# Eight heads instead of four in one visit of the causal value products, with two more exponential tiles on top of rows that are loaded later

## The chip, the cores and the metric

One NeuronCore of a Trainium2 chip runs the whole program. The metric is the device time of one execution in microseconds (us), as the median over several executions.

## What is computed

The reference runs a transformer layer with two attentions and a feed-forward part over 16 batches of 256 tokens of width 256, and then a gated attention. The context has 77 tokens. Everything is float32. Cut to what matters here:

```python
# x: (16, 256, 256), ctx: (16, 77, 256); 16 heads of width 16
h = layernorm(x + multihead(x, x, x, sa_wq, sa_wk, sa_wv, sa_wo, causal=True), ln1_g, ln1_b)
h = layernorm(h + multihead(h, ctx, ctx, ca_wq, ca_wk, ca_wv, ca_wo, causal=False), ln2_g, ln2_b)
ff = relu(h @ ff_w1.T + ff_b1) @ ff_w2.T + ff_b2
x = layernorm(h + ff, ln3_g, ln3_b)
qp, kp, vp = x @ Wq + bq, ctx @ Wk + bk, ctx @ Wv + bv
w = softmax(qp @ kp.T / 16)
out = (w @ vp) * mask * sigmoid(concatenate((qp, w @ vp)) @ Wg + bg) + x
```

The change is in the first line, the causal self-attention: softmax(scores / 16) times the values of each head.

## The kernel before

After a first part (context_products, weights and context) one long program, causal_cross_feed_gated, runs three stages that overlap: the causal attention, the cross attention with the feed-forward part, and the gated attention. Each engine has its own instruction list. All five lists are written by walking the same table `order`, and synchronise by semaphores; an engine never leaves the order of its list. There is no scheduler, so what stands behind a waiting instruction waits too.

The causal stage is cut into iterations n, each of 12 slots s, with the running number g = 12 n + s. A batch has 12 units of scores (line 765 adds the causal mask on the diagonal through an identity, L767 multiplies queries and keys, in bfloat16 parts of float32 numbers) and VectorE takes their row maxima (L1405). Later the scores are computed again, turned (keys on the partitions, L791), with the maximum already in the product; ScalarE takes the exponential (L1168) into one of six tiles pT; GpSimd sets the part above the diagonal to zero (L1819); and TensorE multiplies by the values (L809 and L812, in float32, each head on 32 of the 128 columns, four heads side by side). One such group of four heads is called a visit here. Three units of turned scores feed one visit. The lags in slots between a unit's scores and its turned scores, exponential, zeroing and visit are ST_LAG 20, EXP_LAG 21, SEL_LAG 22 and AV_LAG 25.

In one iteration n, besides the scores of batch n and the turned scores of batches n - 2 and n - 1, these are done:

- slot 1: TensorE turns the maxima (L777); ScalarE and VectorE (L1413, slot 2) write them in two parts into the tile a_mT
- slots 3 to 6: projections of queries and keys of batch n + 2 (L87 with swq, swk). The first waits for L1413, since they share the PSUM tile a_misc
- slot 7: ScalarE copies them (L1139), VectorE takes the remainder (L1420) and GpSimd the rest
- slots 9 and 10: projections of values (L87 with swv), which wait for L1420, since they write over the same PSUM tile
- slots 10 and 11: output projection of batch n - 3 (L87 with swo), with the residual on VectorE (L1447) after it
- slots 5 and 11: VectorE turns the value products back (L1429, then the reciprocal L1431), and later, after a product on GpSimd, L1439

The scores, the turned scores and the visits' results have two PSUM tiles each, so the scores of a slot wait for the maxima of two slots before. Exponential g waits until the visit is done that read its tile last.

SyncE issues the loads in a list of its own: for each batch of the causal stage 12 copies that stack the query and key parts; then for batch c of the cross stage the keys (L674), the values (L682, which wait for the last visits of batch 12 + c, since they lie on the same tiles), the queries (L694) and the feed-forward weights (L687, for c up to 3). Cross slots are put beside the causal ones from iteration 12 on. The norm rows (gains and biases of three layernorms, and ff_b2) are seven tiles of 1 KB per partition, loaded once at the start (L178).

The rule on the tiles, word for word:

```python
act.wait_ge(s_st, g + 1)
atleast(act, s_av, (g - NPT) // 3 + 1)
nc.scalar.activation(pT[g % NPT][:], stps[g % 2][:], ACT.Exp).then_inc(s_exp, 1)
```

Of the kernel before, what the change touches and what calls it, by code (L numbers as in the profile page):

```python
# [5 lines left out]
F32 = mybir.dt.float32  # L6
# [7 lines left out]
P = 128  # L14
# [98 lines left out]
def context_products(nc, ctx, sem, t, a, sw, d):  # L113
# [52 lines left out]
    with nc.Block() as block:  # L166
        @block.sync
        def _(sp):
# [8 lines left out]
            for n, v in t.rows.items():  # L177
                sp.dma_start(v[:], A(n).partition_broadcast(P)).then_inc(small, 16)  # L178
# [27 lines left out]
            sp.wait_ge(small, 16 * (len(t.rows) + len(t.cols) + 1 + 2))  # L206

        @block.tensor
        def _(pe):
# [29 lines left out]
            pe.wait_ge(small, 16 * (len(t.rows) + len(t.cols) + 1 + 2))  # L239
# [237 lines left out]
def causal_cross_feed_gated(nc, ctx, sem, t, wq, wk, wv, wo, x_dram, xT_dram, b1, b2, ln1, ln2, ln3, d, w1_dram, w2_dram, out):  # L477
# [6 lines left out]
    NPT, NVP, NPX, NHID = 6, 4, 4, 3  # L484
    ST_LAG, EXP_LAG, SEL_LAG, AV_LAG = 20, 21, 22, 25
# [11 lines left out]
    pT = [sb(f"pT{i}", [P, 512], F32) for i in range(NPT)]  # L497
# [78 lines left out]
    c_loaded = [sem("feed_weights") for _ in range(4)]  # L576
    c_stacked = [sem("c_stacked") for _ in range(NSTK)]
# [73 lines left out]
    with nc.Block() as block:  # L651
        @block.sync
        def _(sp):
# [57 lines left out]
            for c in range(B):  # L711
# [3 lines left out]
                if c >= NSTK:  # L715
                    load_keys(c)
                    load_values(c)
                load_queries(c)
# [33 lines left out]
        def _(pe):  # L752
# [42 lines left out]
            def values(rr):  # L795
                c, r = divmod(rr, 4)
                if not real(c):
                    return
                j, ro = divmod(r, 2)
                if rr == 0:  # L800
                    pe.wait_ge(v_ones, NVP)
                pe.wait_ge(s_sel, 3 * rr + 3)
                if r == 0:
                    pe.wait_ge(s_vev, c + 1)
                if ro == 0:
                    atleast(pe, s_tr, 2 * (c - 1) + j + 1)
                col = ro * S
                for i in range(4):
                    mt(avps[j][32 * i:32 * i + 32, col:col + S], vpad[c % NVP][:, 0, 4 * r + i, :],  # L809
                       pT[(3 * rr + i // 2) % NPT][:, i % 2 * S:i % 2 * S + S], start=True, stop=False, skip_group_check=True)  # L810
                for i in range(4):
                    last = mt(avps[j][32 * i:32 * i + 32, col + P:col + S], vpad[c % NVP][:, 1, 4 * r + i, :],  # L812
                              pT[(3 * rr + 2) % NPT][:, i * P:(i + 1) * P], start=False, stop=True, skip_group_check=True)
                last.then_inc(s_av, 1)
# [41 lines left out]
            def causal_slot(n, s):  # L856
# [12 lines left out]
                if (g - AV_LAG) % 3 == 0:  # L869
                    values((g - AV_LAG) // 3)  # L870
# [920 lines left out]
        def _(pool):  # L1791
# [71 lines left out]
            def shifted_rows2(c):  # L1863
                if not real(c):
                    return
                pool.wait_ge(c_z2r, c + 1)
# [216 lines left out]
```

## Time and profile before

| | before |
|---|---|
| median of 3 runs | 875.87 us (875.33 to 876.85) |
| profiled execution, device time | 875.57 us |
| its span, first to last instruction | 873.8 us |
| TensorE (PE) busy | 787.0 us, 90% |
| VectorE (DVE) busy | 659.1 us, 75% |
| GpSimd (POOL) busy | 485.5 us, 56% |
| ScalarE (ACT) busy | 438.0 us, 50% |
| mean granted TensorE clock | 0.964 |

Busy shares are averages over the stages. The causal stage fills roughly the stretch from 80 to 390 us of the span; its first value product starts at 110.1 us and its last at 391.2. A granted clock of 1.00 is the 2.4 GHz level of TensorE; a lower mean is a mixture with the 1.2 GHz level. The weight loads of TensorE (PEld) are recorded apart from its products. A float32 product stands as two in the trace, so a visit shows as 8 products of L809 and 8 of L812.

### The profile page before, as it was taken

The page shows a single profiled execution, that of the slowest core. Times are in us where ns is not written, and L with a number is a line of the kernel's source. Part 1 is how long each engine was busy: PE and PEld are TensorE (multiplying, and loading weights), DVE is VectorE, ACT ScalarE, POOL GpSimd, SP SyncE. Part 2 cuts the span into 40 slices and gives each one's busy share as a digit, 9 for nine tenths or more (in the row PEclk, how much of TensorE's full clock was granted, in tenths as well). Part 3 has the DMA queues.
Part 4 walks back from the last instruction along what each step waited for, and adds up shares of the span by engine and source line. Part 5 has one row for each costly group of instructions (what it writes and reads, how often), then busy time and mean ns, then how long its engine had stood idle before and what let it go on. Part 6 is the DMA issues. An engine that isn't in the chain of part 4 may idle for free.

```text
span 873.8 us, 19903 instructions
## 1 busy us (share of the span) xinstructions
PE 787.0 (90%) x7214; PEld 651.1 (75%) x7232; DVE 659.1 (75%) x1498; ACT 438.0 (50%) x907; POOL 485.5 (56%) x598
## 2 busy tenths in 40 slices
PE   5896799999999898788789999999999889999895
PEld 4665677777777675555468888888877789989784
DVE  3545767777777989677989999998888776867863
ACT  4431355555565565556555555555544544444442
POOL 2401466677666676554345666666555775657541
PEclk9999999999999999899789999999999999999987
DMA  8397588768765765346432222222200020012122
GB/s 269 60 356 189 108 132 140 139 118 128 131 115 111 115 105 102 76 88 121 79 72 53 54 52 53 53 53 53 53 2 10 2 77 2 28 54 81 54 81 76
DMA packets 105296, 79.58 MB, mean 91 GB/s; under 512 B 43255, under 2 KB 101961, under 8 KB 104941
## 3 DMA queue, kind: packets, MB, share of 16 engines
q1 hardware_dynamic: 101434, 72.02, 39.9%
q10 hardware_dynamic: 3764, 6.29, 2.0%
q8 instruction: 58, 0.95, 0.5%
q14 instruction: 40, 0.33, 0.1%
HBM read 27.03 MB, written 12.97 MB: 46 GB/s over the span
## 4 chain that ended last, share of the span: by engine, by line
PE 61%; DVE 18%; issue 6%; ACT 3%; SPq 1%; DMA 1%; POOL 1%; POOLq 0%; DVEq 0%; ACTq 0%
PE a_misc L87 14%; PE a_pair L87 11%; PE a_s L1002 8%; PE a_pair L963 3%; PE a_pair L791 3%; PE a_s L767 3%; PE a_pair L948 3%; PE a_pair L809 3%; PE a_s L765 2%; PE a_s L87 2%; PE a_s L925 2%; PE a_pair L1101 2%; DVE a_rest L1420 2%; ACT a_parts L1139 2%; DVE c_z L1509 1%
## 5 line engine op out<-in xcount | busy, mean ns | idle before, releaser
L1405 DVE TENSOR_REDUCE a_nm<-a_s 128x2 f32<-128x512 f32 (+1 forms) x192 | 127.5, 680 | 54.9 <-PE a_s L767 53.3
L1912 POOL TENSOR_TENSOR c_hidden<-c_hid,c_hidden 128x256 fp32r<-128x256 f32 x128 | 95.8, 748 | 118.3 <-DVE c_hid L1647 118.2
L1168 ACT ACTIVATE a_pT<-a_pair 128x512 f32<-128x512 f32 x192 | 113.8, 597 | 93.8 <-PE a_pair L791 87.4
L1263 ACT ACTIVATE a_pT<-a_pair 77x512 f32<-77x512 f32 x128 | 75.9, 593 | 141.9 <-PE a_pair L948 137.5
L1002 PE MATMUL a_s<-c_w,c_hidden 128*128 128x256 f32 x768 | 118.6, 294 | 0.0
L87 PE MATMUL a_pair<-c_fxh,c_w 128*128 128x256 f32 x512 | 101.5, 291 | 12.8 <-DVE c_hid L1647 12.8
L1819 POOL TENSOR_SCALAR_AFFINE_SELECT a_pT<-a_pT 128x256 f32<-128x256 f32 (+1 forms) x192 | 91.1, 492 | 30.2 <-ACT a_pT L1168 29.9
L1002 PEld LDWEIGHTS a_s<-c_w,c_hidden 128*128 128x128 f32 x768 | 99.9, 192 | 0.7 <-issue 0.4
L87 PEld LDWEIGHTS a_pair<-c_fxh,c_w 128*128 128x128 f32 x512 | 80.0, 193 | 15.8 <-DVE c_hid L1647 15.6
L791 PE MATMUL a_pair<-a_sq,a_sk 98*128 98x256 bf16 (+1 forms) x512 | 76.0, 252 | 7.3 <-ACT a_pT L1168 7.1
L1647 DVE TENSOR_SCALAR c_hid<-a_pair,ff_b_col 128x256 f32<-128x256 f32 x128 | 61.3, 479 | 28.0 <-ACT c_hidden L1289 27.9
L767 PE MATMUL a_s<-a_sk,a_sq 96*128 96x256 bf16 (+1 forms) x512 | 74.7, 248 | 4.5 <-DVE a_nm L1405 1.8
L87 PE MATMUL a_pair<-c_fxl,c_w 128*128 128x256 f32 x256 | 72.4, 283 | 0.0
L1571 DVE TENSOR_REDUCE a_nm<-a_s 128x5 f32<-128x385 f32 (+1 forms) x96 | 54.5, 568 | 22.8 <-PE a_s L925 21.9
L1289 ACT ACTIVATE c_hidden<-a_pair,ff_b_col 128x256 fp32r<-128x256 f32 x128 | 59.3, 463 | 7.4 <-PE a_pair L87 7.3
L765 PE MATMUL a_s<-maskb,identb 128*128 128x256 bf16 (+1 forms) x174 | 54.0, 310 | 7.5 <-DVE a_nm L1405 7.5
L767 PEld LDWEIGHTS a_s<-a_sk,a_sq 96*128 96x128 bf16 x512 | 45.6, 99 | 11.1 <-issue 0.6
L948 PE MATMUL a_pair<-a_sq,a_sk 98*77 98x256 bf16 x256 | 51.9, 285 | 1.8 <-ACT a_pT L1263 1.8
L87 PEld LDWEIGHTS a_pair<-c_fxl,c_w 128*128 128x128 f32 x256 | 49.3, 193 | 0.0
L791 PEld LDWEIGHTS a_pair<-a_sq,a_sk 98*128 98x128 bf16 x512 | 35.6, 99 | 15.8 <-ACT a_pT L1168 9.7
L925 PEld LDWEIGHTS a_s<-a_sk,a_sq 96*128 96x128 bf16 x512 | 24.3, 102 | 30.1 <-DVE a_nm L1571 14.3
L1827 POOL TENSOR_TENSOR a_on<-a_tr,a_rc 128x256 f32<-128x256 f32 x32 | 21.2, 661 | 44.2 <-DVE a_rc L1431 44.2
(255 smaller groups left out, 2141.2 us busy)
## 6 DMA issues: line engine op xcount, KB each, us to landing
a_sq<-a_parts SPq DMA_DIRECT2D x96, 128.0 KB, 4.4
a_sk<-a_parts SPq DMA_DIRECT2D x96, 128.0 KB, 4.4
a_sq<-c_parts SPq DMA_DIRECT2D x96, 128.0 KB
x<-in_xT SPq DMA_DIRECT2D x16, 256.0 KB, 5.9
res<-in_x SPq DMA_DIRECT2D x16, 256.0 KB, 5.6
out<-g_fin SPq DMA_DIRECT2D x16, 256.0 KB, 2.1
a_sk<-kc_parts SPq DMA_DIRECT2D x96, 38.5 KB
fold_rows<-x_fold ACTq DMA_DIRECT2D x1, 2496.0 KB, 11.3
```

What stands on the lines that cost most here:

```text
L87: last = pe.matmul(out, a(x, kt), b(y, kt), start=start and n == 0, stop=stop and n == len(seq) - 1)
L765: mt(diag, t.identb[:], t.maskb[:, 0:len(heads), :], start=True, stop=False, skip_group_check=True)
L767: last = mt(out[:, i * w:(i + 1) * w], sq[c % NSTK][0:KS, h, qt * P:(qt + 1) * P], sk[c % NSTK][0:KS, h, 0:w], start=False, stop=True, ski ...
L791: last = mt(stps[g % 2][:, i * w:(i + 1) * w], sk[c % NSTK][:, h, kt * P:(kt + 1) * P], sq[c % NSTK][:, h, q0:S], start=True, stop=True, s ...
L948: last = mt(st_ps[0:SC, i * S:(i + 1) * S], skx[c % NSTK][:, h, :], sq[c % NSTK][:, h, :], start=True, stop=True, skip_group_check=True)
L1002: last = mt(down[:, qt * D:(qt + 1) * D], (hh, hl)[x](m)[:, qt * P:(qt + 1) * P], w2(y, m), start=m == 0 and qt == 0 and i == 0, stop=m == ...
L1168: nc.scalar.activation(pT[g % NPT][:], stps[g % 2][:], ACT.Exp).then_inc(s_exp, 1)
L1263: nc.scalar.activation(pT[g % NPX][0:SC], st_ps[0:SC, :], ACT.Exp).then_inc(c_exp, 1)
L1405: nc.vector.tensor_reduce(nm[c % 2][:, QT * heads[0] + qt:QT * heads[-1] + qt + 1:QT], sps[g % 2][:].rearrange("p (h k) -> p h k", h=len(h ...
L1647: nc.vector.tensor_scalar(hid[n % NHID][:], up[n % 2][:, 0:S], b1[:, m:m + 1], 0.0, ALU.add, ALU.max).then_inc(c_hid, 1)
L1819: nc.gpsimd.affine_select(out=v, in_=v, compare_op=ALU.is_ge, fill=0.0, base=0, pattern=[[0, len(heads)], [1, P]], channel_multiplier=-1). ...
L1912: nc.gpsimd.tensor_tensor(hl(m), hid[n % NHID][:], f32(hh(m)), ALU.subtract).then_inc(c_hl, 1)
```

## The change

Two visits become one. values(p) runs every six slots instead of every three and does eight heads: two groups of four, one right after the other, into the two halves of one PSUM tile. AV_LAG grows from 25 to 28, so that the pair stands where the second of the two visits stood, and the six tiles pT become eight. The two new ones lie on the memory of the rows ln2_b with ln3_g and ln3_b with ff_b2. These four rows are no longer loaded at the start, but by SyncE after the last causal value product, in front of the queries of cross batch 3, and GpSimd waits for them once, in shifted_rows2(0).

```diff
-            for n, v in t.rows.items():
-                sp.dma_start(v[:], A(n).partition_broadcast(P)).then_inc(small, 16)
+            for n in t.first_rows:
+                sp.dma_start(t.rows[n][:], A(n).partition_broadcast(P)).then_inc(small, 16)
...
-    NPT, NVP, NPX, NHID = 6, 4, 4, 3
-    ST_LAG, EXP_LAG, SEL_LAG, AV_LAG = 20, 21, 22, 25
+    NPT, NVP, NPX, NHID = 8, 4, 4, 3
+    ST_LAG, EXP_LAG, SEL_LAG, AV_LAG = 20, 21, 22, 28
...
-    pT = [sb(f"pT{i}", [P, 512], F32) for i in range(NPT)]
+    pT = [sb(f"pT{i}", [P, 512], F32) for i in range(NPT - 2)]
+    pT += [nc.alloc_sbuf_tensor_at(f"a_pT{NPT - 2 + i}", [P, 512], F32, offset=t.place[n]) for i, n in enumerate(("ln2_b", "ln3_b"))]
...
+                if c == NSTK - 1:
+                    sp.wait_ge(s_av, 4 * B)
+                    for v, src in t.later_rows:
+                        sp.dma_start(v[:], src.partition_broadcast(P)).then_inc(rows_loaded, 16)
                 load_queries(c)
...
-            def values(rr):
-                c, r = divmod(rr, 4)
-                if not real(c):
-                    return
-                j, ro = divmod(r, 2)
-                if rr == 0:
+            def values(p):
+                c, j = divmod(p, 2)
+                if not real(c):
+                    return
+                if p == 0:
                     pe.wait_ge(v_ones, NVP)
-                pe.wait_ge(s_sel, 3 * rr + 3)
-                if r == 0:
+                pe.wait_ge(s_sel, 6 * p + 6)
+                if j == 0:
                     pe.wait_ge(s_vev, c + 1)
-                if ro == 0:
-                    atleast(pe, s_tr, 2 * (c - 1) + j + 1)
-                col = ro * S
-                for i in range(4):
-                    mt(avps[j][32 * i:32 * i + 32, col:col + S], vpad[c % NVP][:, 0, 4 * r + i, :],
-                       pT[(3 * rr + i // 2) % NPT][:, i % 2 * S:i % 2 * S + S], start=True, stop=False, skip_group_check=True)
-                for i in range(4):
-                    last = mt(avps[j][32 * i:32 * i + 32, col + P:col + S], vpad[c % NVP][:, 1, 4 * r + i, :],
-                              pT[(3 * rr + 2) % NPT][:, i * P:(i + 1) * P], start=False, stop=True, skip_group_check=True)
-                last.then_inc(s_av, 1)
+                atleast(pe, s_tr, p - 1)
+                for ro in range(2):
+                    rr, col = 2 * p + ro, ro * S
+                    for i in range(4):
+                        mt(avps[j][32 * i:32 * i + 32, col:col + S], vpad[c % NVP][:, 0, 8 * j + 4 * ro + i, :],
+                           pT[(3 * rr + i // 2) % NPT][:, i % 2 * S:i % 2 * S + S], start=True, stop=False, skip_group_check=True)
+                    for i in range(4):
+                        last = mt(avps[j][32 * i:32 * i + 32, col + P:col + S], vpad[c % NVP][:, 1, 8 * j + 4 * ro + i, :],
+                                  pT[(3 * rr + 2) % NPT][:, i * P:(i + 1) * P], start=False, stop=True, skip_group_check=True)
+                    last.then_inc(s_av, 1)
...
-                if (g - AV_LAG) % 3 == 0:
-                    values((g - AV_LAG) // 3)
+                if (g - AV_LAG) % 6 == 0:
+                    values((g - AV_LAG) // 6)
...
+                if c == 0:
+                    pool.wait_ge(rows_loaded, 16 * 4)
...
+        t.first_rows = ("ln1_g", "ln1_b", "ln2_g")
+        t.later_rows = [(t.rows[n], a["L0_xattn_" + n]) for n in ("ln2_b", "ln3_g", "ln3_b", "ff_b2")]
```

The instructions of TensorE's list, slots 7, 8 and the start of 9 of an iteration, before. a_s is the PSUM tile of the scores, a_pair that of the turned scores and of the value products, a_pT an exponential tile, a_vpad the values; the last row is the first value projection:

```order
L765 MATMUL a_s1<-maskb,identb 128x2x128
L767 MATMUL a_s1<-a_sk3,a_sq3 128x256 x2
L791 MATMUL a_pair1<-a_sq1,a_sk1 128x128 x4
L809 MATMUL a_pair1<-a_pT0,a_vpad1 32x256 x2
L809 MATMUL a_pair1<-a_pT1,a_vpad1 32x256 x2
L812 MATMUL a_pair1<-a_pT2,a_vpad1 32x128 x4
L765 MATMUL a_s0<-maskb,identb 128x2x128
L767 MATMUL a_s0<-a_sk3,a_sq3 128x256 x2
L791 MATMUL a_pair0<-a_sq2,a_sk2 128x256 x2
L765 MATMUL a_s1<-maskb,identb 128x2x128
L767 MATMUL a_s1<-a_sk3,a_sq3 128x256 x2
L87 MATMUL a_misc<-swv0,a_xh1 128x256
```

And after (line numbers move by six, the visit's lines are now L814 and L817):

```order
L771 MATMUL a_s1<-maskb,identb 128x2x128
L773 MATMUL a_s1<-a_sk3,a_sq3 128x256 x2
L797 MATMUL a_pair1<-a_sq1,a_sk1 128x128 x4
L771 MATMUL a_s0<-maskb,identb 128x2x128
L773 MATMUL a_s0<-a_sk3,a_sq3 128x256 x2
L797 MATMUL a_pair0<-a_sq2,a_sk2 128x256 x2
L771 MATMUL a_s1<-maskb,identb 128x2x128
L773 MATMUL a_s1<-a_sk3,a_sq3 128x256 x2
L87 MATMUL a_misc<-swv0,a_xh1 128x256
```

The visit of slot 7 is gone from between the turned scores and the scores of the next slot.

TensorE from slot 1 to the first query projection of slot 3, before:

```order
L767 MATMUL a_s1<-a_sk0,a_sq0 128x128 x4
L777 MATMUL a_misc<-ident,a_nm1 128x128
L791 MATMUL a_pair1<-a_sq2,a_sk2 128x128 x4
L809 MATMUL a_pair0<-a_pT0,a_vpad2 32x256 x2
L809 MATMUL a_pair0<-a_pT1,a_vpad2 32x256 x2
L812 MATMUL a_pair0<-a_pT2,a_vpad2 32x128 x4
L765 MATMUL a_s0<-maskb,identb 128x512
L767 MATMUL a_s0<-a_sk0,a_sq0 128x128 x4
L791 MATMUL a_pair0<-a_sq2,a_sk2 128x256 x2
L765 MATMUL a_s1<-maskb,identb 128x512
L767 MATMUL a_s1<-a_sk0,a_sq0 128x128 x4
L87 MATMUL a_misc<-a_xh0,swq0 128x256
```

After:

```order
L773 MATMUL a_s1<-a_sk0,a_sq0 128x128 x4
L783 MATMUL a_misc<-ident,a_nm1 128x128
L797 MATMUL a_pair1<-a_sq2,a_sk2 128x128 x4
L771 MATMUL a_s0<-maskb,identb 128x512
L773 MATMUL a_s0<-a_sk0,a_sq0 128x128 x4
L797 MATMUL a_pair0<-a_sq2,a_sk2 128x256 x2
L771 MATMUL a_s1<-maskb,identb 128x512
L773 MATMUL a_s1<-a_sk0,a_sq0 128x128 x4
L87 MATMUL a_misc<-a_xh0,swq0 128x256
```

Here too the visit is gone, the one of slot 1; the projection follows three rows earlier.

TensorE's list at the visit of slot 4, before:

```order
L791 MATMUL a_pair0<-a_sq2,a_sk2 128x128 x4
L809 MATMUL a_pair0<-a_pT3,a_vpad2 32x256 x2
L809 MATMUL a_pair0<-a_pT4,a_vpad2 32x256 x2
L812 MATMUL a_pair0<-a_pT5,a_vpad2 32x128 x4
L765 MATMUL a_s1<-maskb,identb 128x2x128
```

After:

```order
L797 MATMUL a_pair0<-a_sq2,a_sk2 128x128 x4
L814 MATMUL a_pair0<-a_pT0,a_vpad2 32x256 x2
L814 MATMUL a_pair0<-a_pT1,a_vpad2 32x256 x2
L817 MATMUL a_pair0<-a_pT2,a_vpad2 32x128 x4
L814 MATMUL a_pair0<-a_pT3,a_vpad2 32x256 x2
L814 MATMUL a_pair0<-a_pT4,a_vpad2 32x256 x2
L817 MATMUL a_pair0<-a_pT5,a_vpad2 32x128 x4
L771 MATMUL a_s1<-maskb,identb 128x2x128
```

The place now has two groups of four heads, one behind the other. Slot 10 changes in the same way.

## Rows read from the trace of the kernel before

**Rows 1.** Busy time by stretch (us, count), granted clock (PEclk), share of DMA, GB/s.

```profile
200.00:240.00 40.00, 38.83 (x437) 31.10 (x441) 29.84 (x58) 21.87 (x39) 27.05 (x43) 1.00 0.73 129
...
360.00:400.00 40.00, 30.62 (x356) 20.42 (x354) 26.40 (x64) 22.96 (x46) 20.79 (x31) 0.91 0.46 100
```

**Rows 2.** Line 1420: durations in ns, and who waited for it (us, times).

```profile
L1420 DVE TENSOR_TENSOR a_rest<-a_misc,a_parts x14: 1209/1224/1225, 91.2 to 313.7; 128x1024 f32<-128x1024 f32 x14
...
  PEld a_misc L87: 11.8, 14
```

**Rows 3.** Timeline, iterations 8 and 9: start, us busy, engine, instruction [idle before].

```profile
221.22 0.39 PE L791 MATMUL a_pair<-a_sq,a_sk 98*128 98x256 bf16 x2
...
221.45 0.27 PE L765 MATMUL a_s<-maskb,identb 128*128 128x256 bf16 x1
...
221.65 0.60 ACT L1168 ACTIVATE a_pT<-a_pair 128x512 f32<-128x512 f32 x1 [0.68 <-PE a_pair L791]
...
221.78 0.39 PE L791 MATMUL a_pair<-a_sq,a_sk 98*128 98x128 bf16 x4
...
222.10 0.64 PE L809 MATMUL a_pair<-a_pT,a_vpad 128*32 128x256 f32 x8
222.15 1.02 ACT L1139 ACTIVATE a_parts<-a_misc 128x1024 bf16<-128x1024 f32 x1
...
222.56 0.40 PE L812 MATMUL a_pair<-a_pT,a_vpad 128*32 128x128 f32 x8
...
222.89 0.28 PE L765 MATMUL a_s<-maskb,identb 128*128 128x256 bf16 x1
...
223.20 1.22 DVE L1420 TENSOR_TENSOR a_rest<-a_misc,a_parts 128x1024 f32<-128x1024 f32 x1 [0.52 <-ACT a_parts L1139]
...
224.47 0.39 PE L87 MATMUL a_misc<-swv,a_xh 128*128 128x256 f32 x1 [0.53 <-DVE a_rest L1420]
...
241.97 0.39 PE L87 MATMUL a_misc<-swv,a_xh 128*128 128x256 f32 x1 [0.53 <-DVE a_rest L1420]
```

**Rows 4.** Timeline of TensorE inside the visit at 222.10.

```profile
222.34 0.40 PE L809 MATMUL a_pair<-a_pT,a_vpad 128*32 128x256 f32 x4
...
222.67 0.29 PE L812 MATMUL a_pair<-a_pT,a_vpad 128*32 128x128 f32 x4
```

**Rows 5.** Timeline of TensorE and VectorE, iterations 8 to 11.

```profile
228.53 0.39 PE L767 MATMUL a_s<-a_sk,a_sq 96*128 96x256 bf16 x2
...
228.95 0.69 DVE L1405 TENSOR_REDUCE a_nm<-a_s 128x2 f32<-128x512 f32 x1 [2.20 <-PE a_s L767]
...
232.67 0.28 DVE L1413 TENSOR_TENSOR a_mT<-a_misc,a_mT 32x128 bf16<-32x128 f32 x1
...
233.21 0.47 PE L87 MATMUL a_misc<-a_xh,swq 128*128 128x256 f32 x2
...
268.28 0.28 DVE L1413 TENSOR_TENSOR a_mT<-a_misc,a_mT 32x128 bf16<-32x128 f32 x1
...
268.81 0.47 PE L87 MATMUL a_misc<-a_xh,swq 128*128 128x256 f32 x2 [0.18 <-issue]
```

**Rows 6.** Chain that ended last, 334 to 400 us: start, us, what.

```profile
342.64 3.92 DMA c_raw<-in_L_xattn_ff_w
...
349.15 0.57 PE a_pair L809 x8
...
354.52 0.57 PE a_pair L809 x8
...
370.16 1.01 PE a_pair L809 x8
...
391.05 0.57 PE a_pair L809 x8
```

**Rows 7.** Timeline of SyncE's queue and of TensorE, 390 to 425 us.

```profile
392.82 3.95 SPq L694 DMA_DIRECT2D a_sq<-c_parts  x6
...
408.60 0.40 PE L925 MATMUL a_s<-a_sk,a_sq 96*128 96x77 bf16 x6
```

More of the change, by code:

```diff
@@ L205, in _ @@
                 sp.wait_ge(v, 16)
-            sp.wait_ge(small, 16 * (len(t.rows) + len(t.cols) + 1 + 2))
+            sp.wait_ge(small, 16 * (len(t.first_rows) + len(t.cols) + 1 + 2))
         @block.tensor
@@ L238, in _ @@
             square(1, "wvT", "wg2").then_inc(s_w2, 1)
-            pe.wait_ge(small, 16 * (len(t.rows) + len(t.cols) + 1 + 2))
+            pe.wait_ge(small, 16 * (len(t.first_rows) + len(t.cols) + 1 + 2))
             bq, bk, bv = t.cols["bq"], t.cols["bk"], t.cols["bv"]
@@ L576, in causal_cross_feed_gated @@
     c_loaded = [sem("feed_weights") for _ in range(4)]
+    rows_loaded = sem("later_rows")
     c_stacked = [sem("c_stacked") for _ in range(NSTK)]
```

## The prediction

> **What bounds the kernel now.** I read the table of busy time by stretch first. In the middle of the causal stage TensorE is busy 38.83 of 40 us at full granted clock, VectorE 29.84 [rows 1]. So TensorE carries the stage, and the next question is what its missing microsecond is. The instructions of line 1420 (the remainder a_rest on VectorE, slot 7 of each iteration) answer it: there are 14 of them, one for each iteration 0 to 13, and TensorE's weight loads waited for them 14 times, 11.8 us together, 0.84 us each [rows 2]. The timeline of one iteration (number 8) shows the chain [rows 3]: the turned scores of slot 6 start at 221.22, the exponential of them at 221.65, then ScalarE's L1139 at 222.15, VectorE's L1420 from 223.20 to 224.42, and TensorE's first value projection (slot 9) at 224.47, 0.05 us after its releaser. Nothing in that chain depends on the value visit in slot 7, which lies in the middle of it (222.10 to 222.89). From slot 6's turned scores to slot 9's projection is 3.25 us whatever TensorE does in it: I call it the window.
>
> There is a second coupling, which no list of waits names, and the timeline shows it [rows 5]. VectorE works without a pause from 228.95 (the maxima of slot 11, 0.03 us after the scores they read can be done) through its turn of the value products, reciprocal, residual, the maxima of slots 0 and 1 and the turn back, eight instructions in all, to L1413, 232.67 to 232.95. TensorE's projection in slot 3 needs L1413 and starts at 233.21, 0.26 us after its end. Two iterations on, in number 11, the projection starts at 268.81, again 0.26 us after L1413's end (268.28 + 0.28 = 268.56), and there TensorE, the weights of the first projection included, had plainly been idle. An equal distance where the wait is visible and where it isn't says that the wait binds in both; in iteration 9 it is merely hidden under the last scores. So between slot 11's scores and slot 3's projection TensorE has no slack: its pace is VectorE's.
>
> **What the change does to TensorE.** A visit alone first. Turned scores of 512 columns followed by scores take 0.23 us (221.22 to 221.45); with a visit between them 221.78 to 222.89 is 1.11, so a visit costs 0.88 [rows 3]. Its groups of four start at 222.10, 222.34, 222.56 and 222.67 [rows 3, 4]: a 256-column group 0.22 to 0.24 us, a 128-column one 0.11. The last group holds TensorE 0.22 before the scores start, 0.11 more than it streams, and the first starts 0.09 late (221.78 + 0.23 = 222.01). A second half that follows the first has neither: 0.22 + 0.22 + 0.11 + 0.11 = 0.66 us. A pair in one place thus costs 1.54 where two visits cost 1.76, 0.22 less, and there are 32 pairs: 7.0 us, if TensorE set the pace everywhere.
> The Trainium skill (TensorEngine Tiling (Array Packing), Key Properties) says that changing the tiling mode drains TensorE; the visits use 32-column tiles among full-width work, and by that rule alone the change is a gain of 32 drains. The trace agrees on the drain: it is the 0.09 and the 0.11 above.
>
> But TensorE doesn't set the pace everywhere, and where the visits stood matters. The order shows four visits per iteration before, in slots 1, 4, 7 and 10; after, two double ones in slots 4 and 10.
> Slot 7's visit leaves the window: 0.88 us becomes idle time, nothing is gained.
> Slot 10 gets the second half: scores of slot 11 come 0.66 later, and VectorE's run starts there, so L1413 and the projection of slot 3 come 0.66 later.
> Slot 1's visit lies beside VectorE's run: its 0.88 becomes a wait of TensorE too (in the scores of slots 2 and 3 and the projection of slot 3).
> Slot 4 gets the second half: between slot 3 and the window TensorE sets the pace (VectorE waits for it), so 0.66 again.
> Sum of a regular iteration: 0.66 + 0.66 = 1.32 us longer. Both things removed were hidden, both added are not.
>
> Iterations: value visits run from iteration 2 to 17, the window exists up to 13. In iteration 2 slot 1 and 4 make a pair without a double one in slot 10 before it, and VectorE's run is shorter there (no residual yet): 0.66 - 0.88 = -0.22. Iterations 3 to 12 are regular: 10 x 1.32 = 13.2. In 13 the run of VectorE is longer by the deviations of slot 9 before it and swallows slot 10's half: 0.66. Together 13.6 us up to the window of iteration 13.
>
> After it the cross stage lies beside, and TensorE is busy 30.62 of 40 us at a granted clock of 0.91 [rows 1], so less of it counts. I go by the chain that ended last [rows 6]. It holds second halves to come at 354.52 and 391.05 and one more in iteration 14's slot 10, whose end lets SyncE issue the loads that end in the 3.92 us transfer at 342.64: 3 x 0.66 = +2.0. It holds visits that go: 349.15 (0.88), one more like it in slot 1 of iteration 17 (0.88), and 370.16, which runs at 1.2 GHz, the lower level of the clock (1.01 us for its first part against 0.57), and so about 1.5: -3.3. Slot 10 of iteration 13 adds about 0.4, since VectorE has a long c_z beside it. Sum -0.9; bounds +3.3 (only added halves count, those of slot 10 in iteration 13 and all of the chain's stretches, five of them) and -4 (the removed ones and one more, with no half on the path).
>
> **The other edits.** Tiles: exponential g now waits for the visit of g - 8. For the one right after a double visit's turned scores (slots 5 and 11) that is the first half of that visit, so it starts some 0.9 us later than now; the turned scores that need it come two slots later, with 0.66 of second half, scores and projections between: hidden in the causal stage; iterations 16 and 17 have no projections and may lose some tenths, which I leave to the range.
> Rows: four broadcasts fewer at the start, behind the weights in SyncE's queue; no wait of TensorE there is for them, so nothing. The same four in front of the queries of batch 3: six issues take 3.95 us at 392.82, so four more are 2.6, and the last query rows are issued at 399.4 instead of 396.8, landing some 4 us later (as the transfer of rows 6) at 403.4. The scores that need them start at 408.60 [rows 7]: 5 us of cover, nothing again. If it were gone the cost is up to 2.6. Behind them stand the last feed weights and the keys of batch 4, needed later still. The new wait on POOL is in iteration 4 of the cross stage, past all this. The wait of SyncE for the last value visit is one that its line before already has.
>
> **Sum.** 13.6 - 0.9 = +12.7 on the profiled execution's 875.57: 888.3. The median of the three runs is 0.30 above that execution, so 888.5 for the median.
>
> **Rivals.**
> Only the window binds (0.13). If L1413 isn't what the slot-3 projection waits for, slot 1's visit is a real saving: each of iterations 3 to 13 gets 2 x 0.66 - 0.88 = 0.44, 4.8 in all, less 0.2 and 0.9: 879.5. Against it is the equal 0.26.
> Faster (0.06): the drains decide. If the window shrank with the work in it, the 7.0 us would come in full, 868.8. It decides once the wait for L1420 stays near 0.8 us an iteration instead of growing to 1.7. For it: TensorE at 97% busy. Against it: the chain of the window has no instruction of a visit. This is also what the skill's drain rule gives when it is read alone.
> No change (0.03): VectorE's coupling false and the last iterations at their lower bound: 4.8 - 0.2 - 4 is +0.6, 876.5.
> Slower still (0.08): a second half at a whole visit's price, 0.88, makes an iteration 1.76 longer, 10 of them 17.6, with 0.9 for iteration 13 and -0.9 for the rest 17.6 in all: 893.5; or the late exponentials or the longer idle stretches (1.7 us once per iteration) bring the lower clock, of which the 1.00 in the present rows shows no sign.
> The forecast itself has 0.70, and its own range is 885 to 893 by the bounds of the last part.
>
> **Numbers.** Range: from the window-only case to the price of a whole visit, 879.5 to 893. Runs of this kernel lie within 0.2%, so that is what can be told from no change: slower 0.91, same 0.03, faster 0.06.
>
> **What the new profile would show.** The wait of TensorE for L1420 grows from 0.84 to about 1.7 us in twelve of the fourteen iterations (11.8 + 12 x 0.88 = 22.4 us together). The distance from L1413 to the projection of slot 3 stays 0.26. The projections of slot 9 follow each other at 18.8 us where they now do at 17.5 (224.47 and 241.97 [rows 3]). The second halves start 0.66 after the first. TensorE's waits for a_nm in slots 2 and 3 appear as new rows. I am wrong if the period is 17.9 (window only) or 17.3 (drains), or if cross stage waits name the stacks or the rows.

## The result, and the profile after

The changed kernel takes 890.15 us (median of 4 runs, 889.17 to 896.95) against 875.6 (874.03 to 876.85) for the kernel before, run beside it: a ratio of 1.0177 with a 95% interval of 1.0148 to 1.0207. The profiled execution is one of 889.17 us, span 887.4, at the same mean granted clock as before, 0.964. The forecast was 888.5, and 888.3 for the profiled execution.

Busy time by stretch, same columns as [rows 1]:

```profile
200.00:240.00 40.00, 36.27 (x409) 28.91 (x402) 27.79 (x53) 21.20 (x37) 25.37 (x38) 1.00 0.65 116
```

TensorE is now busy 36.27 of 40 us where it was 38.83, VectorE 27.79 where it was 29.84: at full clock everybody does less in the same time, so what was added is waiting. The line of the remainder (L1425 now), as in [rows 2]:

```profile
L1425 DVE TENSOR_TENSOR a_rest<-a_misc,a_parts x14: 1206/1224/1225, 92.4 to 328.5; 128x1024 f32<-128x1024 f32 x14
...
  PEld a_misc L87: 19.4, 14
  PE a_misc L87: 15.5, 14
```

Two things are to be read here. The wait of the weight loads grew from 11.8 to 19.4 us. And the first and the last start of this line, which runs once in each of iterations 0 to 13, cut the span in three: before 91.2, then 222.5 up to 313.7, then 560.1 to the end of the span; now 92.4, 236.1 and 558.9. The middle part grew by 13.6 us, as much as the whole span; the first part grew by 1.2 and the last shrank by 1.2. The next rows are one iteration on the timeline, the same instructions as in [rows 3]:

```profile
230.10 0.39 PE L797 MATMUL a_pair<-a_sq,a_sk 98*128 98x256 bf16 x2
...
230.53 0.60 ACT L1173 ACTIVATE a_pT<-a_pair 128x512 f32<-128x512 f32 x1 [0.68 <-PE a_pair L797]
...
230.67 0.39 PE L797 MATMUL a_pair<-a_sq,a_sk 98*128 98x128 bf16 x4
...
231.03 1.02 ACT L1144 ACTIVATE a_parts<-a_misc 128x1024 bf16<-128x1024 f32 x1
...
231.61 0.10 PEld L771 LDWEIGHTS a_s<-maskb,identb 128*128 128x128 bf16 x1 [0.24 <-DVE a_nm L1410]
...
232.08 1.23 DVE L1425 TENSOR_TENSOR a_rest<-a_misc,a_parts 128x1024 f32<-128x1024 f32 x1 [0.52 <-ACT a_parts L1144]
...
233.36 0.39 PE L87 MATMUL a_misc<-swv,a_xh 128*128 128x256 f32 x1 [1.24 <-DVE a_rest L1425]
...
252.18 0.38 PE L87 MATMUL a_misc<-swv,a_xh 128*128 128x256 f32 x1 [1.24 <-DVE a_rest L1425]
```

From slot 6's turned scores (230.10) to the projection of slot 9 (233.36) it is 3.26 us, and it was 3.25 with the visit in it. The visit is gone, and the window is as long as it was. The projections are 18.82 us apart (233.36 to 252.18) where they were 17.50. The double visit of slot 4, on TensorE:

```profile
226.33 0.64 PE L814 MATMUL a_pair<-a_pT,a_vpad 128*32 128x256 f32 x8
226.78 0.40 PE L817 MATMUL a_pair<-a_pT,a_vpad 128*32 128x128 f32 x8
227.00 0.61 PE L814 MATMUL a_pair<-a_pT,a_vpad 128*32 128x256 f32 x8
227.43 0.40 PE L817 MATMUL a_pair<-a_pT,a_vpad 128*32 128x128 f32 x8
227.77 0.28 PE L771 MATMUL a_s<-maskb,identb 128*128 128x256 bf16 x1
```

The second half starts 0.67 us after the first (226.33 to 227.00), and the scores behind the pair start at 227.77. VectorE's run ends with L1418, in the same iteration:

```profile
222.47 0.39 PE L771 MATMUL a_s<-maskb,identb 128*128 128x512 bf16 x1 [0.43 <-DVE a_nm L1410]
...
223.39 0.28 DVE L1418 TENSOR_TENSOR a_mT<-a_misc,a_mT 32x128 bf16<-32x128 f32 x1
...
223.93 0.47 PE L87 MATMUL a_misc<-a_xh,swq 128*128 128x256 f32 x2 [0.18 <-issue]
```

223.39 + 0.28 = 223.67, and the projection starts 0.26 later, as in [rows 5]. The scores of slot 2 now show a wait of 0.43 for the maxima of slot 0, where slot 1's visit had stood. In the list of waits from 120 to 330 us that wait and its like have these rows (us, times, longest); the same two rows before, of L765 and L1405, had 3.3 and 0.4 us:

```profile
PEld a_s L771 <- DVE a_nm L1410: 11.8, 25, 1.2
...
PE a_s L771 <- DVE a_nm L1410: 7.8, 14, 1.0
```

### The profile page after: what moved, and what is told of

Same layout as the page of the kernel before. It is cut to its first block, busy times and chain, and to the rows that moved or that the text cites. A ratio compares the mean times of both kernels' runs of the same rounds, so it can differ in the third digit from the quotient of the medians.

```text
span 887.4 us, 19920 instructions
## 1 busy us (share of the span) xinstructions
PE 786.2 (89%) x7232; PEld 652.3 (74%) x7232; DVE 661.8 (75%) x1498; ACT 436.1 (49%) x907; POOL 485.6 (55%) x598
## 3 DMA queue, kind: packets, MB, share of 16 engines
q10 hardware_dynamic: 3764, 6.29, 2.0%
## 4 chain that ended last, share of the span: by engine, by line
PE 58%; DVE 19%; issue 7%; ACT 3%; DMA 2%; SPq 1%; POOL 1%; POOLq 0%; ACTq 0%; DVEq 0%
PE a_misc L87 12%; PE a_pair L87 11%; PE a_s L1007 8%; PE a_pair L968 3%; PE a_pair L814 3%; PE a_pair L797 3%; PE a_pair L953 3%; PE a_s L773 2%; PE a_s L87 2%; PE a_pair L1106 2%; PE a_s L930 2%; PE a_s L771 2%; DVE a_nm L1410 2%; DVE a_rest L1425 2%; DVE a_tr L1434 1%
## 5 line engine op out<-in xcount | busy, mean ns | idle before, releaser
L1824 POOL TENSOR_SCALAR_AFFINE_SELECT a_pT<-a_pT 128x256 f32<-128x256 f32 (+1 forms) x192 | 92.1, 496 | 41.2 <-ACT a_pT L1173 40.9
L771 PE MATMUL a_s<-maskb,identb 128*128 128x256 bf16 (+1 forms) x192 | 60.8, 317 | 14.8 <-DVE a_nm L1410 13.3
L87 PE MATMUL a_misc<-swv,a_xh 128*128 128x256 f32 x128 | 31.5, 311 | 18.6 <-DVE a_rest L1425 15.5
L797 PEld LDWEIGHTS a_pair<-a_sq,a_sk 98*128 98x128 bf16 x512 | 34.2, 99 | 16.9 <-ACT a_pT L1173 10.1
```

What stands on the lines that cost most here:

```text
L87: last = pe.matmul(out, a(x, kt), b(y, kt), start=start and n == 0, stop=stop and n == len(seq) - 1)
L771: mt(diag, t.identb[:], t.maskb[:, 0:len(heads), :], start=True, stop=False, skip_group_check=True)
L797: last = mt(stps[g % 2][:, i * w:(i + 1) * w], sk[c % NSTK][:, h, kt * P:(kt + 1) * P], sq[c % NSTK][:, h, q0:S], start=True, stop=True, s ...
L1824: nc.gpsimd.affine_select(out=v, in_=v, compare_op=ALU.is_ge, fill=0.0, base=0, pattern=[[0, len(heads)], [1, P]], channel_multiplier=-1). ...
```

## The experiments

The diffs are cut to the lines that the argument needs. In the table the middle part runs from the first start of the remainder (VectorE writing a_rest, iteration 0) to its last (iteration 13), and the rest from there to the end of the span, in the profiled execution of each kernel. The period is the distance of two first value projections in the regular iterations. The median of before lay between 874.85 and 876.02 in all comparisons.

| kernel | median us | ratio to before (95%) | middle part | period | rest |
|---|---|---|---|---|---|
| before | 875.6 | | 222.5 | 17.50 | 560.1 |
| changed | 890.15 | 1.0177 (1.0148 to 1.0207) | 236.1 | 18.82 | 558.9 |
| rows_only | 878.19 | 1.0038 (1.0018 to 1.0058) | 222.5 | 17.50 | 557.4 |
| pair_slot4 | 882.55 | 1.0087 (1.0067 to 1.0107) | 231.8 | 18.14 | 555.9 |
| pair_slot10 | 886.49 | 1.0133 (1.0110 to 1.0155) | 229.0 | 18.15 | 562.5 |
| pair_copy_first | 885.37 | 1.0120 (1.0099 to 1.0141) | 229.5 | 18.20 | 561.8 |
| pair_late_turn | 885.75 | 1.0124 (1.0075 to 1.0173) | 231.9 | 18.24 | 557.9 |
| single_copy_first | 867.03 | 0.9897 (0.9858 to 0.9936) | 215.9 | 16.88 | 557.9 |
| single_both | 868.86 | 0.9908 (0.9873 to 0.9944) | 215.5 | 16.81 | 557.5 |
| pair_moved | 880.59 | 1.0058 (1.0028 to 1.0087) | 222.7 | 17.63 | 561.5 |
| rows_only_again | 876.94 | 1.0018 (0.9998 to 1.0037) | 222.6 | 17.50 | 561.0 |
| rows_twice | 879.90 | 1.0040 (1.0018 to 1.0063) | 222.6 | 17.50 | 563.9 |
| rows_behind | 875.65 | 0.9999 (0.9976 to 1.0022) | 222.6 | 17.50 | 558.0 |
| pair_rows_behind | 890.42 | 1.0183 (1.0141 to 1.0224) | 236.0 | 18.81 | 560.4 |

### Which visit was hidden: only one pair of slots merged

pair_slot4 merges slots 1 and 4 and leaves single visits in 7 and 10; pair_slot10 merges 7 and 10 and leaves 1 and 4. Both keep the rows and tiles of the change. values() takes the number of groups as a second argument here. The two edits are written as one below, with j for the number of the merged pair, 0 or 1.

```diff
-                if (g - AV_LAG) % 6 == 0:
-                    values((g - AV_LAG) // 6)
+                rr, off = divmod(g - (AV_LAG - 3), 3)
+                if off == 0 and rr >= 0:
+                    if rr // 2 % 2 != j:
+                        values(rr, 1)
+                    elif rr % 2:
+                        values(rr - 1, 2)
```

> Only the visits of slots 1 and 4 are merged (in slot 4); 7 and 10 stay single. My theory (slot 1's visit is hidden beside VectorE's run up to L1413): every iteration from 3 to 13 is 0.66 us longer, 18.16 us from one L1420 to the next, about 882.5 in all. Rival, only the window binds, or TensorE sets the pace everywhere: 0.66 - 0.88 = -0.22 per iteration, 17.28 us, about 873.

> Only the visits of slots 7 and 10 are merged (in slot 10); 1 and 4 stay single. My theory (slot 7's visit is hidden in the window, slot 10's second half delays VectorE's run): 0.66 us per iteration from 3 to 12, 18.16 us from one L1420 to the next, nothing in iteration 13, about 882 in all. The theory that only the window binds says the same here. Rival, TensorE sets the pace: -0.22 per iteration, 17.28 us, about 873.

pair_slot4, TensorE (slot 2's scores, and two first value projections):

```profile
218.46 0.39 PE L771 MATMUL a_s<-maskb,identb 128*128 128x512 bf16 x1 [0.43 <-DVE a_nm L1418]
...
229.35 0.39 PE L87 MATMUL a_misc<-swv,a_xh 128*128 128x256 f32 x1 [0.53 <-DVE a_rest L1433]
...
247.49 0.39 PE L87 MATMUL a_misc<-swv,a_xh 128*128 128x256 f32 x1 [0.53 <-DVE a_rest L1433]
```

pair_slot10, the same projections:

```profile
229.17 0.38 PE L87 MATMUL a_misc<-swv,a_xh 128*128 128x256 f32 x1 [1.24 <-DVE a_rest L1433]
...
247.32 0.39 PE L87 MATMUL a_misc<-swv,a_xh 128*128 128x256 f32 x1 [1.24 <-DVE a_rest L1433]
```

Each of the two edits makes the iteration 0.65 us longer (18.14 and 18.15), and both together 1.32. So each edit costs one second half, and neither gives back anything for the visit that it takes away. With slot 7's visit in place (pair_slot4) the wait for a_rest is the old 0.53, and slot 2's scores show the new wait of 0.43; with it gone (pair_slot10) it is 1.24. The window-only case had 17.3 for pair_slot4, the drains a gain in both. Both fall. The total of pair_slot10 is above what was expected, 886.5 against 882; its middle part is 6.5 us longer as expected. The later rows (below) may have cost both kernels up to some 2 us, and the rest of its span, 562.5, varies from one execution to the next (last section).

The middle part of pair_slot4 is 2.8 us longer than that of pair_slot10. Its regular iterations don't show this; its last step does, from the projection of iteration 12 to that of 13: 22.93 us, where pair_slot10 has 19.84 and the kernel before 19.80. In that step TensorE's scores waited 1.60 us (309.58) and 0.94 us (312.13) for the maxima, and then it was busy for 6.27 of the 6.4 us from 312.0 to 318.4 at a granted clock of 0.51, so nearly all of the time at the 1.2 GHz level. Such a stretch was not met in the same step of pair_slot10 or of the changed kernel, which wait there too; what brought it on is not shown.

### Making the window shorter: ScalarE's copy ahead of the exponential

In slot 7 ScalarE does the exponential first and then the copy L1139, which is in the window's chain. Here the copy comes first, once in the changed kernel (pair_copy_first) and once in the kernel before (single_copy_first). Nothing is left out.

```diff
+                if s == 7:
+                    part_one(n + 2)
                 exps(U * n + s - EXP_LAG)
                 if s == 2:
                     o_high(n - 3)
-                if s == 7:
-                    part_one(n + 2)
```

> The changed kernel with one line moved: in slot 7 ScalarE copies the projections (L1144) before the exponential of that slot instead of after it. My theory: the window gets shorter by about 0.6 us (the copy could start 0.75 earlier, VectorE's maxima of slot 7 take some of it), in the twelve iterations 2 to 13: 7 us less, about 883, period 18.2. Rival, the window isn't what TensorE waits for but VectorE's or TensorE's load: no change, 890.

> The kernel before with ScalarE's copy L1139 ahead of the exponential in slot 7. My theory: the window of the kernel before has 0.8 us of waiting, and the copy brings 0.6 of it back in twelve iterations: 16.9 us from one L1420 to the next instead of 17.5, about 868 in all. Rival, TensorE at 97% sets the pace: no change, 875.

pair_copy_first, TensorE:

```profile
211.18 0.39 PE L87 MATMUL a_misc<-swv,a_xh 128*128 128x256 f32 x1
...
219.10 0.39 PE L771 MATMUL a_s<-maskb,identb 128*128 128x512 bf16 x1 [0.44 <-DVE a_nm L1410]
...
229.38 0.39 PE L87 MATMUL a_misc<-swv,a_xh 128*128 128x256 f32 x1
```

single_copy_first, busy time of a stretch, and then its timeline:

```profile
200.00:240.00 40.00, 39.89 (x441) 32.25 (x442) 31.67 (x60) 24.04 (x41) 27.77 (x43) 1.00 0.74 130
```

```profile
202.05 1.02 ACT L1139 ACTIVATE a_parts<-a_misc 128x1024 bf16<-128x1024 f32 x1 [0.45 <-PE a_misc L87]
...
202.97 1.08 ACT L1168 ACTIVATE a_pT<-a_pair 128x512 f32<-128x512 f32 x2
...
203.23 1.22 DVE L1420 TENSOR_TENSOR a_rest<-a_misc,a_parts 128x1024 f32<-128x1024 f32 x1
...
204.50 0.39 PE L87 MATMUL a_misc<-swv,a_xh 128*128 128x256 f32 x1
...
221.38 0.39 PE L87 MATMUL a_misc<-swv,a_xh 128*128 128x256 f32 x1
```

The copy (202.05) now begins as soon as the key projections are done and no longer waits behind an exponential, and the remainder is done 0.6 us earlier. The period falls by 0.62 in both kernels, and TensorE's products of slot 9 show no wait for a_rest any more in the regular iterations. In the kernel before that makes TensorE busy for 39.89 of 40 us and the program 1.0% faster, the lowest median of the study (single_both, below, can't be told from it). This is what the window theory had forecast (16.9 us and about 868), and it is reached without any change of the visits. The changed kernel came to 885.37 where 883 was expected; its period of 18.2 was met.

### The other coupling: VectorE's run made shorter

Up to iteration 12 VectorE's turn of the second value products (with its reciprocal) moves from slot 11 to slot 2, behind L1413, and GpSimd's product, the turn back and ScalarE's part of the output move three slots later with it. pair_late_turn is the changed kernel with this, single_both the kernel before with this and with the copy first.

```diff
-                if s == 11:
+                if s == 11 and n - 2 >= LATE:
                     turn_av(n - 2, 1)
...
                 if s == 2:
                     shift_low(n - 1)
+                    if n - 3 < LATE:
+                        turn_av(n - 3, 1)
                 maxes(U * n + s)
```

> The changed kernel, where up to batch 9 VectorE's turn of the second half of the value products (L1429, L1431) comes behind L1413 in slot 2 instead of ahead of the residual in slot 11, and the steps that hang on it come later too. VectorE's run from slot 11's maxima to L1413 gets some 1.4 us shorter. My theory (slot 3's projection waits for that run, which hides slot 1's visit): TensorE is the one that sets the pace there, so an iteration is 0.66 - 0.88 + 0.66 = 0.44 us longer than before the change, 17.94 us from one L1420 to the next instead of 18.82, about 881 in all. Rival, only the window binds: VectorE's run costs nothing and its shortening gives nothing, 18.82 and 890.

> The kernel before with both edits, the copy first and the late turn. My theory: the late turn gives the single visits next to nothing (they fit beside VectorE's run, within some 0.05 us), so 16.85 to 16.9 us an iteration and about 868. Rival, VectorE's run costs the single visits too: clearly below 16.8.

pair_late_turn, TensorE:

```profile
201.85 0.28 PE L772 MATMUL a_s<-maskb,identb 128*128 128x256 bf16 x1 [0.20 <-DVE a_nm L1411]
...
210.26 0.39 PE L87 MATMUL a_misc<-swv,a_xh 128*128 128x256 f32 x1 [1.24 <-DVE a_rest L1426]
...
228.50 0.39 PE L87 MATMUL a_misc<-swv,a_xh 128*128 128x256 f32 x1 [1.24 <-DVE a_rest L1426]
```

0.58 us of each iteration came back (18.82 to 18.24), and 0.88 was expected. That the run of VectorE binds is shown by it; the size is not what I said. 0.20 of the missing 0.30 is seen: the moved turn now stands ahead of slot 2's maxima, and the scores of slot 4 wait for them (201.85, 0.20); the rest I can't place. The median is 885.75 where 881 was expected; in the profiled execution 1.1 us of the excess stands in the step from iteration 12 to 13 (21.62 us where the changed kernel has 20.51), with the granted clock at 0.51 from 312 to 314 us. In single_both the same edit, on top of the copy first, gives 0.07 more in the period, and nothing in the time (868.86 and 867.03, with intervals that overlap): TensorE is full by then, and single visits just fit beside VectorE's run.

### Double visits where they should pay

pair_moved puts the double visits of iterations 2 to 12 in slots 6 and 11, with nine tiles (a few small tiles of the later stages lie on the mask's memory to make room), the copy ahead of the exponential in slot 6, the turns in slots 8 and 2, and single visits from batch 11 on.

```diff
-                if (g - AV_LAG) % 6 == 0:
-                    values((g - AV_LAG) // 6)
+                if s == 6 and 0 <= n - 2 < MOVED:
+                    values(4 * (n - 2), 2)
+                if s == 11 and 0 <= n - 2 < MOVED:
+                    values(4 * (n - 2) + 2, 2)
+                if (g - 25) % 3 == 0 and (g - 25) // 3 >= 4 * MOVED:
+                    values((g - 25) // 3, 1)
```

> Double visits for batches 0 to 10 in slots 6 and 11 instead of 4 and 10, with nine tiles (two of them on the later rows), the copy ahead of the exponential of slot 6 and the turns in slots 8 and 2; single visits for the last five batches. Both double visits now lie where something else sets the pace: one in the window, one beside VectorE's run. My theory: slots 4 and 10 lose 0.88 each, slot 11 gets 1.54 and slot 1 loses 0.88, so that stretch is 1.1 us shorter; the window is some 0.1 us shorter: 16.3 us from one L1420 to the next, twelve times 1.2 less, about 864 in all with the later rows' cost of up to 3. Rival, double visits are bad for their bursts wherever they stand (late exponentials, late maxima): 17.5 or more.

```profile
204.54 0.28 PE L773 MATMUL a_s<-maskb,identb 128*128 128x256 bf16 x1
...
205.08 0.69 DVE L1419 TENSOR_REDUCE a_nm<-a_s 128x2 f32<-128x512 f32 x1 [1.89 <-PE a_s L775]
...
205.69 1.22 DVE L1434 TENSOR_TENSOR a_rest<-a_misc,a_parts 128x1024 f32<-128x1024 f32 x1
...
206.96 0.39 PE L87 MATMUL a_misc<-swv,a_xh 128*128 128x256 f32 x1 [0.63 <-DVE a_rest L1434]
...
224.59 0.38 PE L87 MATMUL a_misc<-swv,a_xh 128*128 128x256 f32 x1 [0.62 <-DVE a_rest L1434]
```

The period is 17.63 and not 16.3, the median 880.59 and not 864: this expectation was wrong. The rows, of TensorE and VectorE, show where. The scores of slot 7 stand behind the double visit of slot 6 on TensorE (204.54), so VectorE's maxima of slot 7 start at 205.08 after 1.89 us of waiting, and the remainder, whose copy on ScalarE had ended at 203.99, stands behind these maxima in VectorE's list (205.69). From slot 6's turned scores at 202.78 to the projection at 206.96 the window is 4.18 us, where it is 2.64 in single_copy_first (201.86 to 204.50): longer by the 1.54 of a pair. A pair placed in the window doesn't stay out of its chain if a maximum that stands ahead of the remainder needs the scores behind the pair. Whether another order of VectorE would bring the gain of the pairs was not tried.

### The rows by themselves

rows_only is the kernel before, with single visits and six tiles, and only the edit on the rows: four of them loaded behind the last value product. rows_only_again is the same kernel once more. rows_twice has all seven at the start and the four a second time later. rows_behind has the four behind the queries and the feed-forward weights of batch 3 instead of in front of them, and pair_rows_behind is the changed kernel with that:

```diff
+                load_queries(c)
+                if c < NSTK:
+                    load_feed_weights(c)
                 if c == NSTK - 1:
                     sp.wait_ge(s_av, 4 * B)
                     for v, src in t.later_rows:
                         sp.dma_start(v[:], src.partition_broadcast(P)).then_inc(rows_loaded, 16)
-                load_queries(c)
-                if c < NSTK:
-                    load_feed_weights(c)
```

> The kernel before with the later rows alone: six tiles, a visit every three slots. My theory: nothing, 875.6 us within 0.2%, the first use of the later rows and the query stacks of batch 3 both covered. Rival: the four broadcasts in SyncE's queue delay the cross stage, up to 2.6 us more; or the 1 us that the changed kernel lost ahead of the causal stage comes from the shorter list at the start, which would show here as a first value projection about 1 us later.

> The same kernel as the one with the rows moved, run again beside it on the same chip: 877 to 879 us as before, the remainder of iteration 0 ends near 94 us.

> The kernel before with all seven rows loaded at the start as before, and four of them loaded a second time in front of the queries of cross batch 3, with GpSimd's wait: the later loads alone, without the shorter list at the start. If the 3 us of the kernel with the rows moved come from the shorter start (other timing of the first products and a lower clock at 66 to 92 us), this one is at the time of before, 875 +- 1 us, and the remainder of line 1420 ends in iteration 0 at 92.4 us of the span as before. If the later loads cost it (they delay the queries of batch 3), it is at 878, with the start as before and the loss after 392 us.

> The kernel with the rows moved and single visits, but the four row loads stand behind the queries and the feed-forward weights of cross batch 3 instead of in front of them. All traces with the loads in front show one wait of TensorE of about 2 us that those without don't: turned scores at 401 us wait for the 16 KB copy of a_mT that ScalarE's queue issued at 395.0, while the row loads had been issued at 392.7 to 394.9. If these loads hold that copy up, the wait is gone (0, or under 0.5) and the time is that of before, 875.3 +- 1. If the cost of the later rows is the four further transfers wherever they stand, the wait stays or another one of 2 us takes its place, and the time stays at 877 to 880.

> The changed kernel with the same edit. By the first theory its wait of 2.2 us for the copy of a_mT (turned scores at 414.5) is gone and the time falls by about 2 us from 890.15, to 888, so that only the visits' cost is left; by the second it stays at 890.

The edit that I had costed at nothing costs 1.6 to 3.3 us when it stands alone, by the medians of the two comparisons (the interval of the second, 0.9998 to 1.0037, just takes in no change). One explanation was the shorter list at the start, since rows_only starts its first remainder at 92.9 and the kernel before at 91.2. It fell twice: rows_only_again starts it at 90.9, ending at 92.1 and not near 94 as expected, and rows_twice has the long list at the start and is as slow. It is the later loads. In the kernel before, the copy of the maxima a_mT into a_sq, issued from ScalarE's queue, is in time; the turned scores that need it wait for an exponential:

```profile
395.21 0.53 ACTq L1254 DMA_DIRECT2D a_sq<-a_mT  x1
...
400.46 0.38 PE L948 MATMUL a_pair<-a_sq,a_sk 98*77 98x256 bf16 x2 [1.14 <-ACT a_pT L1263]
```

In rows_only_again the row loads are issued just ahead of that copy:

```profile
392.65 0.81 SPq L722 DMA_DIRECT2D ln_b<-in_L_xattn_ln_b  x1
...
394.45 0.43 SPq L722 DMA_DIRECT2D ff_b<-in_L_xattn_ff_b  x1
...
395.04 0.53 ACTq L1259 DMA_DIRECT2D a_sq<-a_mT  x1
...
401.33 0.65 PE L953 MATMUL a_pair<-a_sq,a_sk 98*77 98x256 bf16 x2 [2.17 <-DMA a_sq<-a_mT]
```

The same turned scores now wait 2.17 us for the copy, which was issued at 395.04, right after the last of four broadcasts of 128 KB each, and start 6.29 us after its issue where they started 5.25 after it (1.04 us later). In rows_behind the loads are issued after the copy:

```profile
396.41 0.53 ACTq L1259 DMA_DIRECT2D a_sq<-a_mT  x1
...
401.65 0.38 PE L953 MATMUL a_pair<-a_sq,a_sk 98*77 98x256 bf16 x2 [1.14 <-ACT a_pT L1268]
```

5.24 us again, the wait for the exponential again, and the time is that of before (0.9999). A wait of TensorE for that copy, of 1.35 to 2.85 us, stands in all nine traces with the loads ahead of the queries, and in none of the five with the loads behind them or at the start. That the copy was held up by the broadcasts is thus shown; that it accounts for the whole 1.6 to 3.3 us is not, since the visible place costs 1.04 and the executions also differ in clock (granted from 400 to 405 us: 0.66 before, 0.55 in rows_only_again, 0.83 in rows_behind).

In the changed kernel the same cure takes the wait away: the turned scores start 5.24 us after the copy's issue (409.80 to 415.04) instead of 6.35 (408.16 to 414.51). The median doesn't show it, 890.42 where about 888 was expected, against 890.15 without the cure. The interval of pair_rows_behind is 1.0141 to 1.0224, some 7 us wide, so an effect of 1 to 2 us can be neither seen nor ruled out there.

## Why the prediction was right

**The window.** Shown. Its length stayed (3.26 us), and the projections of slot 9 are 18.82 us apart where 18.8 was forecast. Taking 0.6 us out of its chain took 0.62 out of the period.

**VectorE's run.** Shown. The distance from the end of L1413 (L1418 now) to the projection stayed 0.26; pair_slot4 found slot 1's visit worth nothing; and a shorter run gave 0.58 back. The equal distance, with and without a visible wait, was the sign to go by.

**The second half at 0.66 us.** 0.67 on the timeline, and 0.65 in the period for each of the two merged pairs. The Trainium skill (TensorEngine Tiling (Array Packing), Key Properties) says that a change of tiling mode drains TensorE, and the trace agrees: the pair, from the end of its turned scores' 0.23 us to the next scores, takes 227.77 - 226.23 = 1.54 us, where two single visits took 1.76. By that rule alone the change is a gain of 32 drains, 7.0 us at the 0.22 of these rows. The saving is there where a pair stands on the timeline (the busy time of the whole program, 787.0 us before and 786.2 after, doesn't resolve it), and the program is slower by twice as much, since what left was in places where TensorE waited anyway. One sign named in the prediction was sized wrongly: with two pairs an iteration the drains alone would give a period of 17.5 - 0.44 = 17.1, not 17.3; the measured 18.82 is far from both.

**The sum up to iteration 13.** 13.6 us forecast; the middle part is 236.1 where it was 222.5, so 13.6. Its parts agree too. By the distances of the first value projections, the step into iteration 2 got 0.25 us shorter (0.22 forecast), the ten regular ones 13.1 longer together (13.2), and the step into iteration 13 got 0.71 longer (0.66).

**The rest.** -0.9 forecast, -1.2 measured from the last remainder to the end, with +1.2 ahead of the first one, which wasn't forecast. Neither can be taken as shown: rows_only and rows_only_again, the same kernel, differ by 2.0 us in the first part and 3.6 in the last. That the total of the profiled execution came within 0.9 us of the forecast is in this part luck.

**The wait for L1420.** 22.4 us was forecast, and 19.4 is what the weight loads show (a growth of 7.6 instead of 10.6). The step was mis-sized: I took all of slot 7's visit to appear as wait of the projection, in twelve iterations. TensorE's product waits 1.24 where it waited 0.53, 0.71 more and not 0.88; the remaining 0.17 is in the scores of slot 9, which now come early enough to wait for the maxima of slot 7 (231.61, 0.24). In the regular iterations the idle time is thus the same, but spread over two rows. And it is not twelve times 0.71: in iteration 10 the wait grew by 0.49 only (0.53 to 1.02), and in iteration 12 by 0.05 (0.57 to 0.62).

**The late exponentials.** They came, and they were hidden in the causal stage as forecast. From 120 to 330 us ScalarE's exponentials waited for the visits (us, times, longest):

```profile
ACT a_pT L1173 <- PE a_pair L817: 40.0, 22, 2.3
```

No row of TensorE's waits in that stretch names an exponential tile. So the rule on the tiles is not what made the period longer.

**The other edits at nothing.** Wrong by itself, too small to be seen in the sum. The cover that I had looked at was that of the queries of batch 3, and they were in time: the first scores of batch 3 (423.50) show no wait. I had not looked at who else issues transfers in those microseconds. In the changed kernel:

```profile
406.95 4.06 SPq L696 DMA_DIRECT2D a_sq<-c_parts  x6
...
408.16 0.53 ACTq L1259 DMA_DIRECT2D a_sq<-a_mT  x1
...
414.51 0.65 PE L953 MATMUL a_pair<-a_sq,a_sk 98*77 98x256 bf16 x2 [2.24 <-DMA a_sq<-a_mT]
...
423.50 0.40 PE L930 MATMUL a_s<-a_sk,a_sq 96*128 96x77 bf16 x6
```

The queries are issued from 406.95, and what waits is the turned scores of batch 1, for the copy of its maxima from ScalarE's queue. By the prediction's own sign ("if cross stage waits name the stacks or the rows") this step was wrong, since a_sq is one of the stacks. The forecast of the total had the term at nothing, and what it cost inside the changed kernel is not known beyond the 1.1 us at that place.

**The rivals.** Window only, drains and no change all fell with the period. The case of a whole visit's price for a second half (a period of 19.3) fell too. The lower clock did not come in the changed kernel: its granted clock is 1.00 from 200 to 330 us, as before. It did come once, in iteration 13, in pair_slot4 and in pair_late_turn.

## What to carry to other kernels

Before work is merged on the engine that is busiest, look at each place it leaves and each place it goes to: what left a stretch whose length another engine's chain sets was free there, and what goes to a stretch that the engine sets itself is paid in full. Such a chain can be found where no wait is shown, by the distance from the end of the supposed releaser to the start of the waiting instruction: here it was the same where the wait was visible and where it wasn't, and the experiments showed that it bound in both. The cheaper cure was to take one instruction out of the way of that chain, here by swapping two instructions on an engine that is half idle.
For a transfer that is moved, price the small copies of other queues that will be issued behind it, not only those in its own list.

## What the runs showed that I had not expected

The same kernel gives other times for its first 92 us. Line of the remainder in rows_only and in rows_only_again:

```profile
L1425 DVE TENSOR_TENSOR a_rest<-a_misc,a_parts x14: 1208/1225/1226, 92.9 to 315.4; 128x1024 f32<-128x1024 f32 x14
```

```profile
L1425 DVE TENSOR_TENSOR a_rest<-a_misc,a_parts x14: 1208/1225/1225, 90.9 to 313.5; 128x1024 f32<-128x1024 f32 x14
```

2.0 us apart at the first start, with 222.5 and 222.6 us between first and last. The granted clock from 80 to 92 us was 0.76 in the one and 0.86 in the other, with TensorE busy 9.85 and 7.57 us there; which came first, the lower clock or the later start of the work, is open. The middle part of the span is 222.5 or 222.6 us in all five traces with the single visits and the copy of before, while the first and last parts differ by 2 to 4 us from one execution to the next, along with the clock; across its runs the kernel before lay between 872.71 and 881.29 us, wider than the three runs of the table ahead of the prediction showed. For a change in this stage the period on the timeline tells more than the total: 0.65 us an iteration stood out in a single trace.
